# Hyperbolic self attention through logarithms on ScalarE, and two earlier copies in the first cross stage

## What is computed

```python
q_norm_sq = jnp.sum(q * q, axis=-1, keepdims=True)
k_norm_sq = jnp.sum(k * k, axis=-1)[:, :, None, :]
qk = jnp.einsum('bhnd,bhmd->bhnm', q, k)
diff_sq = jnp.maximum(q_norm_sq + k_norm_sq - 2.0 * qk, 0.0)
denom = jnp.maximum((1.0 - q_norm_sq) * (1.0 - k_norm_sq), 1e-06)
cosh_arg = jnp.maximum(1.0 + 2.0 * diff_sq / denom, 1.0)
distance = jnp.arccosh(cosh_arg)            # 0 where cosh_arg is 1
attn = jax.nn.softmax(-distance, axis=-1)
out = jnp.einsum('bhnm,bhmd->bhnd', attn, v)
```

## Time and profile before

| | |
|---|---|
| median of 3 runs | 6829.18 us (6828.07 to 6832.04) |
| the profiled execution | 6834.64 us, span 6832.6 us |
| busy of the span | PE 85%, PE weight loads 67%, VectorE 56%, ScalarE 41%, GpSimd 26% |
| mean granted TensorE clock | 0.914 of full speed |
| L0_xattn | about us 79 to 1100 of the span |
| L3_attn | about us 5577 to 6053 of the span |

### The profile page before, as it was taken

How to read it: one execution, slowest core, us unless ns; L and a number is a source line. 1 busy time by engine, 2 the same in 40 slices (tenths; PEclk the granted TensorE clock), 3 DMA queues, 4 the chain that set the end, 5 groups by cost and what they waited for, 6 DMA issues and landing times.

```text
span 6832.6 us, 164751 instructions
## 1 busy us (share of the span) xinstructions
PE 5811.0 (85%) x54018; PEld 4560.4 (67%) x54018; DVE 3824.7 (56%) x12136; ACT 2818.7 (41%) x6643; POOL 1796.7 (26%) x2870
## 2 busy tenths in 40 slices
PE   6999998888679999988888999766689988888888
PEld 5777776777447776666666777654467777766666
DVE  5666664444336665644444666664456669954444
ACT  2444442111234442254544555334445532245555
POOL 3555552000013332200000333850024433310000
PEclk9999998999779998999998999888789988889999
DMA  3000000000000000000000101000001100000000
GB/s 131 17 17 18 17 17 6 0 0 0 0 16 29 30 28 0 0 0 0 0 0 6 35 31 31 1 0 0 0 26 34 32 12 0 0 0 0 0 0 12
DMA packets 43768, 93.48 MB, mean 14 GB/s; under 512 B 7696, under 2 KB 28560, under 8 KB 42640
## 3 DMA queue, kind: packets, MB, share of 16 engines
q1 hardware_dynamic: 43664, 92.09, 4.2%
HBM read 88.92 MB, written 3.15 MB: 13 GB/s over the span
## 4 chain that ended last, share of the span: by engine, by line
issue 45%; PE 41%; DVE 7%; ACT 3%; POOL 3%; POOLq 0%; DVEq 0%; DMA 0%; SPq 0%; ACTq 0%
PE psum_banks L548 5%; PE psum_banks L553 4%; PE psum_banks L613 3%; PE psum_banks L1602 3%; PE psum_banks L657 3%; PE psum_banks L664 3%; PE psum_banks L617 2%; PE psum_banks L1578 2%; PE psum_banks L1637 2%; PE psum_banks L1076 1%; DVE scratch L1805 1%; PE psum_banks L1064 1%; PE psum_banks L1620 1%; PE psum_banks L1031 1%; DVE scratch L920 1%
## 5 line engine op out<-in xcount | busy, mean ns | idle before, releaser
L2274 PE MATMUL psum_banks<-w_L_ffn_up,x_normed_T 128*128 128x352 f32 (+3 forms) x2112 | 879.0, 539 | 96.9 <-DVE x_normed_T L2416 63.4
L263 POOL TENSOR_TENSOR ln_vareps<-ln_meanvar,ln_eps 128x1 f32<-128x1 f32 x165 | 44.6, 270 | 2801.0 <-DVE ln_meanvar L258 2801.0
L780 DVE TENSOR_REDUCE scratch<-psum_banks 128x2 f32<-128x514 f32 x768 | 530.7, 691 | 407.2 <-PE psum_banks L548 403.8
L699 ACT ACTIVATE scratch<-psum_banks 128x512 f32<-128x512 f32 x768 | 458.6, 597 | 490.7 <-PE psum_banks L558 485.3
L2312 ACT ACTIVATE scratch<-psum_banks 128x176 f32<-128x176 f32 (+3 forms) x1120 | 398.6, 371 | 620.2 <-PE psum_banks L2274 530.4
L553 PE MATMUL psum_banks<-scratch 32*128 32x128 f32 x6144 | 639.8, 310 | 8.1 <-ACT scratch L699 6.1
L548 PE MATMUL psum_banks<-scratch 32*128 32x257 f32 x3072 | 570.2, 438 | 51.5 <-DVE scratch L781 51.4
L2252 PEld LDWEIGHTS psum_banks<-consts,scratch 128*128 128x128 f32 x2144 | 279.0, 153 | 442.8 <-issue 288.1
L2260 PE MATMUL psum_banks<-w_L_ffn_down,scratch 128*128 128x128 f32 x4096 | 557.3, 282 | 10.3 <-ACT scratch L2303 10.3
L2274 PEld LDWEIGHTS psum_banks<-w_L_ffn_up,x_normed_T 128*128 128x128 f32 x2112 | 411.9, 220 | 229.9 <-issue 112.9
L2456 DVE SCALAR_TENSOR_TENSOR scratch<-scratch,psum_banks 128x176 f32<-128x176 f32 (+2 forms) x704 | 257.5, 373 | 527.0 <-ACT scratch L2312 484.0
(11 more groups left out here) (429 smaller groups left out, 14315.8 us busy)
## 6 DMA issues: line engine op xcount, KB each, us to landing
scratch<-in_ctx SPq DMA_DIRECT2D x99, 514.0 KB, 3.5
scratch<-in_ctx_rows SPq DMA_DIRECT2D x130, 128.0 KB, 2.0
w_L_ffn_up<-in_L_ffn_up SPq DMA_DIRECT2D x1, 2992.0 KB, 9.8
w_L_ffn_down<-in_L_ffn_down SPq DMA_DIRECT2D x1, 2112.0 KB, 12.0
w_L_ffn_up<-in_L_ffn_up SPq DMA_DIRECT2D x1, 2080.0 KB, 7.9
x_tokens<-in_x SPq DMA_DIRECT2D x1, 2048.0 KB, 8.0
scratch<-last_values SPq DMA_DIRECT2D x128, 8.0 KB
out<-x_tokens SPq DMA_DIRECT2D x1, 2048.0 KB, 6.3
```

What stands on the lines that cost most here:

```text
L699: act.activation(pT[:, b % 2, 2 * h:2 * h + 2].rearrange("p t c q -> p t (c q)"), W, ACT.Exp).then_inc(exp_ready.sem, 1)
L780: dve.tensor_reduce(parts[:, r.t.odd, 2 * h:2 * h + 2, 0, b], S, X_AXIS, ALU.max, negate=True)
L2274: pe.matmul(U[g % 3][:, 0:fw * halves], k.xnT[:, :], up[:, c0:c0 + fw * halves], start=True, stop=True).then_inc(sg["up_written"].sem, 1)
```

## The change

In L3_attn the two square roots become Ln and then Exp with scale 0.5 (D gets a bias of 1e-24, a one-column tile `tiny`, so that the logarithm of zero is not asked for). The weights are formed as logarithms: R = ln E - 2 ln(sqrt D + sqrt S), minus the maximum of its row, and an Exp on ScalarE writes `pr`. VectorE loses both reciprocals and both products after them, and gets a scalar-tensor-tensor and an addition. ScalarE loads one function table at the start of the stage. ScalarE does Relu, Ln and Exp of tile t before `take_turned(t-1)`, and `take_qkv` before, `take_heads` after the new Exp. PE does `turn(t)` before `output(t-1)` where it did it after.

In L0_xattn PE does `z_turn(r, 2)` before the second `turn` of step 2 and ScalarE does its `z_out` before the first exponentials of that step; in step 0 ScalarE copies `queries(r, 3)` before the first exponentials.

```diff
-                            "S": [P, 512], "sD": [P, 512], "R": [P, 512]}}[kind])
+                            "S": [P, 512], "sD": [P, 512], "R": [P, 512], "tiny": [P, 1]}}[kind])
...
-        return (["E"] * has.own + ["rr", "w"] * has.turned + ["R", "RE", "max", "nm"] * has.own + ["stats"] * has.third)
+        return (["E"] * has.own + ["rr", "w"] * has.turned + ["R", "max"] * has.own + ["stats"] * has.third)
...
+            if kind == "L3" and r.own:
+                turn(r.t)
             if r.turned:
                 output(r.t + -1)
-            if kind == "L3" and r.own:
-                turn(r.t)
...
-            if r.turned:
+            if kind != "L3" and r.turned:
                 take_turned(r.t + -1)
             if kind == "L3":
...
                     act.wait_ge(d_ready.sem, d_ready.at(r.t, 1))
-                    act.activation(s["sD"], s["D"], ACT.Sqrt)
+                    act.activation(s["sD"], s["D"], ACT.Ln, bias=s["tiny"]).then_inc(log_step.sem, 1)
+                    act.wait_ge(log_step.sem, log_step.at(r.t, 1))
+                    act.activation(s["sD"], s["sD"], ACT.Exp, scale=0.5)
+                if r.turned:
+                    take_turned(r.t + -1)
+                if r.own:
                     act.wait_ge(scores_read.sem, scores_read.at(r.t, 1))
-                    act.activation(s["S"], s["S"], ACT.Sqrt).then_inc(roots.sem, 1)
+                    act.activation(s["S"], s["S"], ACT.Ln).then_inc(log_step.sem, 1)
+                    act.wait_ge(log_step.sem, log_step.at(r.t, 2))
+                    act.activation(s["S"], s["S"], ACT.Exp, scale=0.5).then_inc(roots.sem, 1)
                 if r.after:
                     take_x(r.t + 2)
                 if r.own:
+                    act.activation(s["R"], s["E"], ACT.Ln)
                     act.wait_ge(root_sum.sem, root_sum.at(r.t, 1))
-                    act.activation(s["S"], s["sD"], ACT.Square).then_inc(squared.sem, 1)
+                    act.activation(s["S"], s["sD"], ACT.Ln).then_inc(logs_ready.sem, 1)
+                if r.after:
+                    take_qkv(r.t + 2)
+                if r.own:
+                    act.wait_ge(shifted.sem, shifted.at(r.t, 1))
+                    act.wait_ge(turned_written.sem, turned_written.at(r.t + -1, 1))
+                    act.activation(heads_first(s["pr"]), batches_first(s["R"]), ACT.Exp).then_inc(probs_ready.sem, 1)
                 if r.turned:
                     take_heads(r.t + -1)
-                if r.after:
-                    take_qkv(r.t + 2)
...
+        if kind == "L3":
+            act.preload_act_table_set("natural_log_exp_and_others")
+            act.wait_ge(set_up.sem, set_up.at(1))
         plan.run(act, one)
...
-                dve.wait_ge(squared.sem, squared.at(r.t, 1))
-                link(dve.reciprocal(s["R"], s["S"]), r, "R")
-                link(dve.tensor_tensor(s["R"], s["R"], s["E"], ALU.mult), r, "RE")
-                link(dve.tensor_reduce(s["rs"], s["R"].rearrange("p (u k) -> p u k", k=32), X_AXIS, ALU.max), r, "max")
-                link(dve.reciprocal(s["nm"], s["rs"]), r, "nm")
-                dve.wait_ge(turned_written.sem, turned_written.at(r.t + -1, 1))
-                dve.tensor_tensor(heads_first(s["pr"]), batches_first(s["R"]),
-                                  bc(s["nm"].rearrange("p (b t) -> p b t", b=NB), 3, 32), ALU.mult
-                                  ).then_inc(probs_ready.sem, 1)
+                dve.wait_ge(logs_ready.sem, logs_ready.at(r.t, 1))
+                link(dve.scalar_tensor_tensor(s["R"], s["S"], -2.0, s["R"], ALU.mult, ALU.add), r, "R")
+                link(dve.tensor_reduce(s["nm"], s["R"].rearrange("p (u k) -> p u k", k=32), X_AXIS, ALU.max, negate=True), r,
+                     "max")
+                dve.tensor_tensor(s["R"].rearrange("p (u k) -> p u k", k=32), s["R"].rearrange("p (u k) -> p u k", k=32),
+                                  bc(s["nm"], 2, 32), ALU.add).then_inc(shifted.sem, 1)
...
@@ null_key_attention, PE
+                if b == 2:
+                    z_turn(r, b)
                 turn(r, b, 1)
                 if b == 0:
                     last_weights(r)
-                if b == 2:
-                    z_turn(r, b)
...
@@ null_key_attention, ScalarE
-                if b == 1:
+                if b == 1 or b == 2:
                     z_out(r, b)
                 if b == 3:
                     queries(r, 0)
+                if b == 0:
+                    queries(r, 3)
                 exponentials(r, b, 0)
                 turned(r, b)
-                if b == 0:
-                    queries(r, 3)
...
-                if b != 1:
+                if b == 0 or b == 3:
                     z_out(r, b)
```

More of the change, by code:

```diff
@@ L913, in self_attention @@
     else:
-        sq_ready, d_ready, roots, root_sum, squared = (
-            PerTile(k.sig(n), 1) for n in ("squares_ready", "distance_ready", "roots_ready", "root_sum", "root_sum_squared"))
+        sq_ready, d_ready, log_step, roots, root_sum, logs_ready, shifted = (
+            PerTile(k.sig(n), m) for n, m in (("squares_ready", 1), ("distance_ready", 1), ("log_ready", 2), ("roots_ready", 1),
+                                              ("root_sum", 1), ("root_sum_log", 1), ("log_weights_shifted", 1)))
         wq, wk, wv, wo = (k.load(f"L3_attn_W{n}", [P, P]) for n in "qkvo")
@@ L1368, in dve @@
         if kind == "L3":
+            dve.memset(s["tiny"], 1e-24)
             dve.tensor_copy(s["qbd"][:, 1, :].rearrange("p (b j q) -> p b j q", b=NB, j=4),
```

## The result

The changed kernel takes 6726.5 us in the median of four runs (6716.73 to 6742.24), the kernel before 6830.61 us on the same chip: a ratio of 0.985, interval 0.983 to 0.9869. That is 104 us less; forecast were 94.5 us less (6735, range 6702 to 6785). The interval of the ratio means 90 to 116 us.

What follows compares the result with a forecast made beforehand. VectorE's order was taken to pace L3_attn at 14.63 us per tile. Gains of 78 us there and 16.5 in L0_xattn, 94.5 together, took the profiled 6834.64 us to 6740, a median of 6735, range 6702 to 6785.

Steps and rivals of the forecast that it cites:

- The sum: Whole kernel: 78 us less from L3_attn plus 16.5 from L0_xattn, 94.5 us together.
- VectorE's operations: L3_attn: 4.98 us removed per tile, two new operations at 0.69 us each, net 3.60 less, giving 11.03 us.
- The new wait: L3_attn: VectorE's residual waits 0.9 us for output behind turn, mostly where GpSimd held VectorE up anyway.
- The walk: L3_attn: step-by-step timing of one tile through the engines, counted from the end of VectorE's new addition.
- VectorE's path of 11.3 us: L3_attn: VectorE's order gives 11.3 us per tile; TensorE has 0.3 us slack at full clock.
- The clock: L3_attn: each 3.4 us at half clock loses 1.7 us of work; 12.2 us per tile taken, between 11.3 and 13.4.
- Rival 2: L3_attn: TensorE's chain operands, scores, heads, turn, output, residual at half clock sets 13.4 us per tile; 6778 us, chance 0.20.
- step 2: L0_xattn: earlier z_turn and z_out gain nothing in full-clock rounds, only clock falls, 17 us at most, 8.5 taken.
- step 0: L0_xattn: copying queries 3 first saves 0.25 to 0.35 us per round, 8 us at 0.25.
- The term taken at half its worth: L0_xattn: 12 clock falls of 1.43 us behind the wait before next_null, 17 us at most, 8.5 taken.
- Rival 1: L3_attn: the clock rises and VectorE alone sets 11.3 us per tile; 6703 us, chance 0.17.
- Rival 3: L3_attn: ScalarE reloads function tables six times per tile between Ln and Exp, 16.3 us per tile; 6865 us, chance 0.05.

Runs made afterwards that it cites:

- the kernel with both edits: Changed kernel with take_turned moved first on ScalarE and the weight-sum products made 128 columns wide in L3_attn: 6680.65 us, ratio 0.9778.
- `take_turned` first: Changed kernel with the previous tile's take_turned ahead of Relu, Ln and Exp on ScalarE in L3_attn: 6678.95 us, ratio 0.9781.
- The four best versions: Changed kernel with take_turned first (6678.95 us), 128-column sums (6681.77), both (6680.65), or those sums with output before turn (6682.69).

## Why the prediction was right, and where not

**The sum.** 94.5 us forecast, 104 measured. By profile L3_attn gave 65 us between its first and last tile and 2.5 behind it, where 78 were taken, and L0_xattn 32 where 16.5 were. Two errors of opposite sign, 10 us short and 16 over, so that the total is closer than its parts: that much is luck.

**VectorE's operations.** Right: 0.68 and 0.69 us for 0.69 each. But "14.63 - 3.60 = 11.03 if nothing else comes up" was not what VectorE did: the holding by GpSimd went too, and it is busy about 9.1 us per tile.

**The new wait.** Placed right (the residual, behind `turn` and `output`), sized wrong: 2.9 us for 0.9. The walk let `turn` start when the weights were ready; TensorE comes 3 us later in the round shown.

**VectorE's path of 11.3 us.** This is the step that failed. It was taken as the lower end that half clock would lengthen, with a slack of 0.3 us on TensorE. In the changed kernel VectorE waits every round, 2.9 us, and no instruction of VectorE is in the chain that ended last from us 5590 to 5840: TensorE's order sets the pace, with its waits of 0.43 and 0.36 us for ScalarE's copies. The walk let the scores start when VectorE's operands are ready, 7.2 us after the new addition. In the round shown above the operands are ready at 5706.3 and the scores start at 5709.42: TensorE is the late one.

**The clock.** The forecast charged one visit to half clock of 3.4 us per tile, and half of its loss. Measured are 3.5 us per tile in the middle of the stage (0.86 is 28% at half clock) and 4.2 over all its periods, a loss of 1.8 to 2.1 us of work. The nearest row for the loop at full clock is 10.85 us, from the kernel with both edits; it is another kernel, and VectorE is in its chain. If it stands for the changed kernel too, an estimate, 12.58 - 10.85 = 1.73 us are lost, so nearly the whole loss shows and not half. A loop 0.45 us shorter and a loss 0.8 us dearer than forecast nearly cancelled: 12.2 for 12.5. So the chosen value was good by two errors of opposite sign. Rival 2 named the right engine, not the right chain: in the changed kernel the scores never wait for VectorE's operands between us 5590 and 5840, and its 13.4 us assumed more half clock than came.

**L0_xattn.** The mechanisms held: the stall moved to the next `z_turn` and a full-clock round gained nothing from step 2 (31.52 us), step 0 gave 0.42 us for 0.25. The term taken at half its worth, 8.5 us of clock falls, should have stood at its full 17: all of them went. The half was a choice with no row behind it, and why all of them go is still open.

**Rival 1**, a denser order raising the clock by itself, was not there in the changed kernel. With `take_turned` first the clock came (0.97) and the period with it (10.99 us), but VectorE did not set it alone: it still waits 1.5 us per tile. **Rival 3** is real for a kernel without the line that names the table; with it there is one load.

## What to carry to other kernels

Where TensorE's clock moves between its two levels, an order's waits can't be priced by their length: the same stage took 12.6, 11.6, 11.1 or 11.0 us per tile with nearly the same work. Which order raises the clock was found by running it; no rule came out of these runs. After an engine is relieved, walk the chain again from the engine that now sets the pace, and test thin products and single short waits there first. Name the function table when Ln and Exp alternate, and look for the loads in the instruction list.

The four best versions, at 6679 to 6683 us, beat the changed kernel by some 0.7% (0.978 against 0.985) and can't be told from each other; the simplest is `take_turned` first.

## What the runs showed of the hardware

- Making 4-column products 128 columns wide made the stage faster: clock 0.86 to 0.97, 12.58 to 11.14 us per tile, with TensorE busy for the same 232 of 250 us.
- Moving one ScalarE copy, for which TensorE waited 0.43 us per tile, did the same: clock 0.86 to 0.97, 12.58 to 10.99 us per tile.
- Alternating products of 128 rows and of one row costs 0.42 us per pair of records; with 128 rows in both it is 0.22 us, at full clock. A one-row product is no saving there.
- A faster TensorE step made the tile slower (10.85 to 11.49 us). VectorE's product with both inputs in SBUF went from 0.68 to 1.19 us in the mean beside GpSimd's products, and the scores' wait for it grew by 0.5 us per tile, most of the difference; the clock is also lower (0.97 for 1.00). No run holds the clock and lets only the product change.
- Without the named table, ScalarE loads a table of 1.28 us at each change between Ln and Exp, 191 in the stage; with it, one.
- Unchanged stages took 888 to 903 us with the same instructions in different kernels, and the time at half clock goes with it (262 us of 890.5, 289 of 903.3).
